# Weights rounded onto the e4m3 grid by TensorE in PSUM instead of by GpSimd and VectorE

## The reference

```python
u = jnp.einsum('bsd,hd->bsh', x, W_in) + b_in            # x: layernorm of the input
def step(state, u_t):
    s = jnp.tanh(u_t + state * gamma + beta)
    return (s, s)
_, states = jax.lax.scan(step, init, jnp.swapaxes(u, 0, 1))
y = jnp.einsum('bsh,dh->bsd', states, W_out) + b_out
...
def _quantized_matmul(x, w, scale):
    wq = w.astype(jnp.float8_e4m3fn).astype(x.dtype)
    y = jnp.einsum('bsi,io->bso', x, wq)
    return y * scale
gate = jax.nn.silu(_quantized_matmul(x, gate_w, gate_scale))
up = _quantized_matmul(x, up_w, up_scale)
return _quantized_matmul(gate * up, down_w, down_scale)
...
x = x + _layernorm(_L0_attn_ref(_layernorm(x), ...))
x = x + _layernorm(_L0_ffn_ref(_layernorm(x), ...))
```

## Time and profile before

| | |
|---|---|
| median of 3 runs | 625.39 us (625.18 to 625.69) |
| the profiled execution | 625.78 us, its span 624.0 us |
| TensorE busy | 528.8 us, 85% |
| VectorE busy | 481.0 us, 77% |
| ScalarE busy | 310.6 us, 50% |
| GpSimd busy | 240.4 us, 39% |
| mean granted TensorE clock | 0.937 |

### The profile page before, as it was taken

The page is one execution under the profiler, slowest core; times in us unless marked ns, Lnnn a source line. Parts: engine busy times, 40 slices in busy tenths (PEclk is TensorE's granted clock), DMA queues, the critical chain, the costliest instruction groups (busy, mean ns, idle before and its releaser), DMA issues.

```text
span 624.0 us, 9844 instructions
## 1 busy us (share of the span) xinstructions
PE 528.8 (85%) x2880; PEld 449.0 (72%) x2880; DVE 481.0 (77%) x1832; ACT 310.6 (50%) x1442; POOL 240.4 (39%) x320
## 2 busy tenths in 40 slices
PE   4655232878999999999999999999999992999993
PEld 4644211568977998789878987799779971798992
DVE  4999997999778667966787679767886678675734
ACT  1354423365554755576546654665466544452330
POOL 2776672555224222422333332422342224243532
PEclk9957757789999999999999999999999996999997
DMA  7453440301010200110012001100001000100000
GB/s 235 128 171 123 124 141 29 90 29 52 1 35 1 69 1 1 35 67 2 1 34 69 1 2 34 56 14 0 2 3 65 2 0 2 67 2 2 1 35 34
DMA packets 16598, 27.47 MB, mean 44 GB/s; under 512 B 2336, under 2 KB 4512, under 8 KB 16544
## 3 DMA queue, kind: packets, MB, share of 16 engines
q1 hardware_dynamic: 16544, 26.84, 13.7%
HBM read 22.63 MB, written 4.19 MB: 43 GB/s over the span
## 4 chain that ended last, share of the span: by engine, by line
DVE 57%; ACT 21%; PE 14%; issue 3%; DMA 1%; SPq 1%; POOL 1%; POOLq 0%; DVEq 0%; ACTq 0%
DVE recur L634 23%; ACT pairs L922 10%; PE gate_up L528 7%; ACT pairs L909 4%; DVE fused L728 4%; ACT sigm L942 4%; DVE gated L721 3%; PE wide L553 3%; DVE peaks L780 3%; ACT fused_hi L957 3%; PE wide L493 2%; DVE rounder_own L776 2%; DVE y L675 2%; DVE z L793 2%; DVE x_in L658 2%
## 5 line engine op out<-in xcount | busy, mean ns | idle before, releaser
L922 ACT ACTIVATE pairs<-recur 128x16 f32<-128x16 f32 x1024 | 191.2, 187 | 249.5 <-DVE recur L634 247.1
L634 DVE TENSOR_TENSOR_SCAN recur<-recur,pairs 128x32 f32<-128x32 f32 x1024 | 234.4, 229 | 101.5 <-ACT pairs L922 100.1
L1025 POOL TENSOR_TENSOR fused_lo<-fused,fused_hi 128x256 fp32r<-128x256 f32 x96 | 71.1, 741 | 180.5 <-ACT fused_hi L957 180.4
L468 PE MATMUL wide<-x_norm_t,w_in_sb 128*128 128x256 f32 x448 | 106.6, 396 | 17.5 <-ACT pairs L909 13.2
L482 PE MATMUL wide<-w_out_sb,pairs 128*128 128x512 f32 x224 | 101.3, 606 | 22.1 <-DMA w_out_sb<-w_out_t 22.1
L468 PEld LDWEIGHTS wide<-x_norm_t,w_in_sb 128*128 128x128 f32 x448 | 87.6, 199 | 34.6 <-ACT pairs L909 15.4
L482 PEld LDWEIGHTS wide<-w_out_sb,pairs 128*128 128x128 f32 x224 | 65.5, 297 | 51.8 <-DMA w_out_sb<-w_out_t 22.5
L528 PE MATMUL gate_up<-x_hi,gate_q 128*128 128x256 f32 x384 | 96.8, 285 | 1.0 <-DVE fused L728 0.6
L528 PE MATMUL gate_up<-x_lo,up_q 128*128 128x256 f32 x384 | 96.0, 283 | 0.0
L528 PE MATMUL gate_up<-x_hi,up_q 128*128 128x256 f32 x384 | 95.6, 282 | 0.0
L528 PE MATMUL gate_up<-x_lo,gate_q 128*128 128x256 f32 x384 | 94.9, 281 | 0.0
(11 more groups left out here) (75 smaller groups left out, 640.2 us busy)
## 6 DMA issues: line engine op xcount, KB each, us to landing
x_in<-x SPq DMA_DIRECT2D x16, 256.0 KB, 3.1
x_res<-x SPq DMA_DIRECT2D x16, 256.0 KB, 3.1
out<-z SPq DMA_DIRECT2D x14, 256.0 KB, 2.4
raw_own<-gate_w SPq DMA_DIRECT2D x10, 256.0 KB, 2.8
raw_own<-down_w SPq DMA_DIRECT2D x9, 256.0 KB, 2.7
w_in_sb<-w_in_t SPq DMA_DIRECT2D x4, 512.0 KB, 6.8
raw_own<-up_w SPq DMA_DIRECT2D x8, 256.0 KB, 2.7
w_out_sb<-w_out_t SPq DMA_DIRECT2D x8, 256.0 KB, 2.9
```

The lines of the kernel that those rows point to most:

```text
L468: ins = eng.matmul(wide[bank][:, jj * TOK:(jj + 1) * TOK], w_in_sb[:, k, j * P:(j + 1) * P], x_norm_t[:, k, :], start=(k == 0), stop=(k == ...
L634: eng.tensor_tensor_scan(preact[:, part(h), :].rearrange("p c k -> p (c k)"), factors[:, part(h), :].rearrange("p c k -> p (c k)"), pairs[ ...
L922: eng.activation(pairs[:, (n * T + t) % RING, part(h), 0], preact[:, part(h), 1], ACT.Tanh).then_inc(s_state[h], 1)
L1025: eng.tensor_tensor(fused_lo[:, f, :], fused[:, f, :], fused_hi[:, f, :].bitcast(F32), ALU.subtract).then_inc(s_fused_lo, 1)
```

## The change

R is made by VectorE as before, but from `powers` (two slots in the memory of `x1`) into a float32r `rounder`. The rounding itself goes to TensorE: `round_weights` adds three products in one PSUM bank, identity x raw piece in float32, identity x R and minus identity x R in float32r (`signed_ident`, written once by ScalarE). ScalarE copies the bank to the weights in two halves (`take_weights`), at `TAKE_BEHIND` = 4 and 5 places behind the matmuls' place, which is 1.5 behind the piece's fourth VectorE place. Three banks take turns. A raw slot is loaded again when TensorE has done its piece. VectorE keeps four instructions for every piece, GpSimd none. Pieces 0 to 3 now stand in the prologue (their matmuls at places 0 to 0.3 of block 0), 4 to 32 in block 0 and 33 to 35 in block 1 (VectorE places 1 to 21); the guard on gate and up moves to places 32 to 35 of block 1 and that on down to 39, 40, 43, 49. With the same rule for free places, piece 4 has VectorE places 1, 2, 3, 6, piece 5 has 7, 11, 12, 13, piece 6 has 14, 15, 20, 21, and from 22 on each piece has four places in a row up to 125.

```diff
-        PIECES_START, PIECES_FIRST = 6, 27
+        PIECES_START, PIECES_FIRST = 4, 33
...
-                piece_at[i] = [next(slots) for _ in range(4 if by_pool(i) else 8)]
+                piece_at[i] = [next(slots) for _ in range(4)]
...
-        GUARD_GATE_UP = [next(second_slots) for _ in range(4)]
         lay_pieces(PIECES_FIRST, NP, second_slots)
-        GUARD_DOWN = [next(second_slots) for _ in range(4)]
+        free = [s for s in second_slots if s >= GUARD]
+        GUARD_GATE_UP, GUARD_DOWN = free[0:4], free[4:8]
+
+        def round_place(i):
+
+            return piece_at[i][3] + 1.5 if i >= PIECES_START else 0.1 * i
...
-                    if i >= RAW and by_pool(i - RAW):
-                        eng.wait_ge(s_pool_converted, pool_pieces(i - RAW + 1))
-                    elif i >= RAW:
-                        eng.wait_ge(s_dve_converted, 2 * (i - RAW + 1 - pool_pieces(i - RAW + 1)))
+                    if i >= RAW:
+                        eng.wait_ge(s_rounded, i - RAW + 1)
...
+            def round_weights(first, end):
+
+                for i in range(first, end):
+                    yield round_place(i)
+                    bank = round_banks[i % NRB]
+                    if i == 0:
+                        eng.wait_ge(s_signed_ident, 2)
+                    eng.wait_ge(s_rounder, 4 * i + 4)
+                    if i >= NRB:
+                        eng.wait_ge(s_converted, 2 * (i - NRB + 1))
+                    eng.matmul(bank, ident[:, :], raw[i % RAW], start=True, stop=False)
+                    eng.matmul(bank, signed_ident[:, 0, :], rounder[i % RAW], start=False, stop=False)
+                    eng.matmul(bank, signed_ident[:, 1, :], rounder[i % RAW], start=False, stop=True
+                               ).then_inc(s_rounded, 1)
...
                 if n == 0:
                     strands.append(project_first_u(1, FIRST_U["u"]))
+                    strands.append(round_weights(0, PIECES_FIRST))
...
+            def take_weights(first, end):
+                for i in range(first, end):
+                    for half in range(2):
+                        yield round_place(i) + TAKE_BEHIND + half
+                        if half == 0:
+                            eng.wait_ge(s_rounded, i + 1)
+                        eng.copy(pieces[i][1][:, halves(half)], round_banks[i % NRB][:, halves(half)]
+                                 ).then_inc(s_converted, 1)
```

More of the change, by code:

```diff
@@ L69 @@
 CHAIN_BEHIND = 0.6
+GUARD = 30
+TAKE_BEHIND = 4
 LAG = 3
@@ L185, in recurrent_sandwich_kernel @@
         raw = [raw_own[:, r, :] for r in range(OWN)] + [z[:, 0, :]]
-        rounder = [rounder_own[:, r, :] for r in range(OWN)] + [z[:, 1, :]]
+        rounder = [rounder_own[:, r, :] for r in range(OWN)] + [
+            fused_lo[:, 0:2, :].rearrange("p f t -> p (f t)")]
+        powers = [x1[:, r, :] for r in range(2)]
+        signed_ident = fused_hi[:, 0, :].rearrange("p (s c) -> p s c", s=2)
         stats = {w: sb(f"stats_{w}", [P, batch, 2, nc.vector.BN_STATS_DIM]) for w in "xyrz"}
@@ L257, in recurrent_sandwich_kernel, with last_rounded_in @@
         s_last_ready = sem("s_last_ready")
[L259 to L266, removed]
+        round_banks = [gate_up[NG - 1][:, :, :].rearrange("p v t -> p (v t)"), wide[2][:, :], wide[3][:, :]]
+        NRB = len(round_banks)
+        def last_rounded_in(bank):
+            return max(i for i in range(NP) if i % NRB == bank) + 1
         def halves(h):
@@ L537, in down_products @@
                 if n == 0:
[L538 to L542, removed]
+                    eng.wait_ge(s_converted, 2 * (GATE_UP_PIECES + i + 1))
                     if i == DOWN_IN_TIME:
@@ L783, in convert @@
                     eng.wait_ge(s_rounder, 4 * i + 3)
[L784 removed]
+                    eng.tensor_scalar(rounder[i % RAW], powers[i % 2], LEAST_NORMAL, ROUNDING_CONSTANT, ALU.max,
                                       ALU.mult).then_inc(s_rounder, 1)
[L786 to L794, removed]
[L795 to L800 removed]
             def guard_weights(which, places, first, end, poisoned):
@@ L816, in guard_weights @@
                 eng.wait_ge(s_guard_step, 4 * which + 3)
-                eng.wait_ge(s_dve_converted, 2 * (end - pool_pieces(end)))
+                eng.wait_ge(s_converted, 2 * end)
                 eng.scalar_tensor_tensor(out=poisoned, in0=guard[:, 2:3], scalar=0.0, in1=poisoned.bitcast(F32),
@@ L957, in high_parts @@
                     eng.copy(fused_hi[:, f, :], fused[:, f, :]).then_inc(s_fused_hi, 1)
-            weave(warm_up(), *[copy_x(0, b, FIRST_BEFORE) for b in range(batch)], first_u(0, FIRST_BEFORE["u_copy"]))
+            weave(warm_up(), sign_identity(), *[copy_x(0, b, FIRST_BEFORE) for b in range(batch)], first_u(0, FIRST_BEFORE["u_copy"]))
             for n in range(NB):
@@ L1044, in tail @@
                 return strands
-            def round_weights(first, end):
-                for i in range(first, end):
-                    if not by_pool(i):
-                        continue
-                    yield piece_at[i][3]
-                    src, dst = raw[i % RAW], pieces[i][1]
-                    eng.wait_ge(s_rounder, 4 * i + 4)
-                    eng.tensor_tensor(src, src, rounder[i % RAW], ALU.add).then_inc(s_pool_rounded, 1)
-                    eng.wait_ge(s_pool_rounded, pool_pieces(i) + 1)
-                    eng.tensor_tensor(dst, src, rounder[i % RAW], ALU.subtract).then_inc(s_pool_converted, 1)
-            weave(prepare(), *[root("x", 0, b, FIRST_BEFORE["x_whole"][b]) for b in range(batch)],
-                  round_weights(0, PIECES_START))
+            weave(prepare(), *[root("x", 0, b, FIRST_BEFORE["x_whole"][b]) for b in range(batch)])
             for n in range(NB):
```

38 lines of the change are left out of this document (20 added, 18 removed).

## The result

| | before | after |
|---|---|---|
| median | 625.38 us (625.14 to 625.84, 10 runs) | 627.19 us (626.75 to 628.55, 10 runs) |
| ratio of the medians | | 1.0032, 95% interval 1.0024 to 1.0040 |
| the profiled execution | 625.78 us, span 624.0 us | 627.5 us, span 625.7 us |
| TensorE, VectorE busy | 528.8 and 481.0 us | 573.7 and 447.2 us |
| ScalarE, GpSimd busy | 310.6 and 240.4 us | 330.0 and 166.8 us |

The account below looks back on a forecast made before the run. The bound was the recurrence between VectorE and ScalarE, lengthened by GpSimd's rounding. From 625.8 us, -3.3 for gains less TensorE queue waits, +3.6 for half clock, +0.3 for longer first matmuls: 626.0 us, range 621.5 to 631.0.

Parts of the forecast that it names:

- first scan: Start of block 0: scan 0 at 21.2 us, when ScalarE's copies of the first inputs end, 4.6 us earlier.
- step 6: Block 0: piece 3 waits for its bank behind ScalarE's copies, so scan 7 starts at 31.8; 2.0 us lost.
- projections, steps 51, 55, 63, 71: Block 0: ScalarE's copies wait for pieces queued on TensorE among block 1's input projections; 9.2 us in all.
- steps with two ScalarE copies: Block 0, places 74 to 77: four input copies meet two weight copies, costing 0.3 us.
- block 1, step 12: y: Block 1: block 0's first product y stands before piece 33 on TensorE, whose copy is late; 2.9 us lost.
- block 1, guard: Block 1, places 32 to 35: weight guard beside a GpSimd residual add; 0 to 0.93 us, taken as 0.5.
- block 1, GpSimd's exit: Block 1: without GpSimd's rounding the longer steps shrink from 8.7 to 1.75 us, so 7.0 us go.
- that rival: VectorE writes float32r at half rate, 9 us more over 29 instructions in block 0: 635 us; chance 0.05.
- three pauses: TensorE idle before pieces 3, 6 and 35; half clock after each 7 in 10, costing 1.6, 1.9, 1.9 us.
- The forecast's case: Two of TensorE's three pauses are followed by the half clock, 3.6 us: range 624 to 628 us, chance 0.36.
- The second rival (clock up): TensorE's clock stays up through the pauses: 622.4 us; chance 0.22.
- One mark: Block 0's sign of a wrong forecast: waits of ScalarE for TensorE under 12 us in all.

Follow-up runs that it names:

- the last run: The changed kernel run once more, unchanged, which gave its second profile: 627.15 us, ratio 1.0032.
- the kernel with all moved: Against the kernel with projections apart and later copies: fifth slot, copies of pieces 0 to 3, second group's quads, y and last two pieces' copies moved; 606.64 us, ratio 0.9705.

## Why the prediction was right or wrong

The forecast was 626.0 us, with 621.5 to 631.0 around it, and slower as the likeliest sign; it came out at 627.19. The mechanism was the one forecast, and most of the long steps stand where they were put. But that the total is off by only 1.2 us is partly luck: without the clock, the sum was 622.8 us for the profiled execution (625.8 - 3.3 + 0.3), where 627.5 less the clock's 1.25 is 626.2; it was 3.4 us too low, and the clock took 2.3 less than the 3.6 I gave it. Each term, in the profiled execution (us above a plain step where it is a step):

| step of the prediction | worked out | measured |
|---|---|---|
| first scan | at 21.2 | at 22.25 |
| 128 plain steps | 61.6 | 61.9 |
| the 14 long steps gone | all | all |
| step 1: piece 4's load | 5.2 | 5.03 |
| step 6 | 2.0 | 2.26 |
| step 12: quad before piece 4 | 1.7 | 1.72 |
| projections, steps 51, 55, 63, 71 | 2.0 + 2.8 + 2.2 + 2.2 = 9.2 | 2.18 + 2.66 + 2.11 + 1.80 = 8.7 |
| steps with two ScalarE copies | 0.3 | 1.7 (ten) |
| step 26, block 0 | 0.2, 1.9 more at half clock | 1.5; 0.27 with the pause filled |
| block 1, step 0 | 0 | 1.0 |
| block 1, step 12: y | 2.9 | 2.1 |
| block 1, transposes and copies | 0.4 | 0.6 |
| block 1, guard | 0.5 | 0 |
| block 1, GpSimd's exit | -7.0 | -6.2 |

**Right.** That GpSimd held VectorE: shown by the kernel without its rounding (of the amount that I let go with it, the 0.1 us of step 127 stays in every kernel). That the same amount would come back as waits for TensorE, place by place: the six steps of block 0 that wait for a piece came within 0.4 us each, from nothing but durations and the order in the program. Scan 2 was to start at 27.4 and started at 28.25, the late first scan included. That writing float32r costs VectorE nothing: 0.41 us for L809, so that rival fell.

**Mis-sized.** First, the start: 21.2 took the copies' end from a trace in which it didn't matter. The first scan of the kernels with the change came between 20.93 and 22.32 us. In this profile the first quads took 6.67 us, where the kernel before shows 5.73 in the same place (first after, then before):

```profile
9.64 6.67 PE L457 MATMUL wide<-x_norm_t,w_in_sb 128*128 128x128 f32 x32 [0.74 <-ACT x_norm_t L904]
9.51 5.73 PE L449 MATMUL wide<-x_norm_t,w_in_sb 128*128 128x128 f32 x32 [0.80 <-ACT x_norm_t L879]
```

Within these 32 records the matmuls first follow each other at 0.21 us, then at 0.11. The change of pace comes at 15.6 us here and at 13.5 in the kernel before, and over the kernels with the change the first scan goes with it: at 20.93 to 21.07 us where 13 or 14 records come 0.21 apart, at 22.25 to 22.32 where 25 or 26 do. It isn't that the weights come late, as I expected before the last run: TensorE waits for none of them in this profile, and in one of the others only (0.24 us). Matmuls of this shape are 0.21 us apart in the second profile too where the granted clock is 0.50, but here the clock's record says 1.00, so what sets the pace at the start stays open. In the kernel before, VectorE's work on pieces 4 and 5 lay over it. Second, ScalarE: I looked for weight copies beside input copies only at 74 to 77, though the earlier trace rows show what two copies do to a step. The other eight steps (19, 20, 27, 28, 52, 60, 67, 68) are at 0.15 to 0.19 each; the kernel with one product has the same ten. Third, the last piece's two copies have place 130.5, beyond the block, and were emitted right behind the block's last tanh, before TensorE was done:

```profile
105.52 0.40 PE L518 MATMUL wide<-rounder_own,fused_hi 128*128 128x512 f32 x1
...
105.95 0.65 ACT L891 CAST down_q<-wide 128x256 fp32r<-128x256 f32 x2 [0.57 <-PE wide L518]
```

I had taken a place as something that runs on from block to block; it cost 1.0 us, and the kernel with all moved, whose last copies stand in block 1, doesn't have it. The other way went y (0.8 less than worked out) and the guard: its one-element instructions were not held beside GpSimd at all, so of my 0 to 0.93 the nothing was right.

**The clock.** I gave each of three pauses 7 in 10 and 1.6 to 1.9 us. The prices held roughly: 1.6 for the first (0.6 and 1.0 on two steps), 0.8 to 1.3 for the second, 1.5 for the third. How many fall isn't fixed by the program: one in one profile, three in the other. The forecast's case, two of them, was in neither. Over the seven profiles of kernels with such pauses (the kernel after twice, the pause before piece 6 filled, copies later, a fifth slot, and the two with projections apart), those of 2.59 to 2.71 us were followed by the half clock in 7 cases of 10 and those of 2.27 and 2.28 in 3 of 7, so the chance that I gave was about right for the first two and high for the third, which came out at 2.28 us and not 2.5. With one, my sum gives 622.8 + 1.9 = 624.7 us for that execution, and it took 627.5. The missing 2.8 us are the start (1.05), the double copies (1.4), block 1's step 0 (1.0), less gained by GpSimd's exit (0.8) and 0.5 behind block 1, together 4.75; against them stand y (0.8), the guard (0.5) and the clock's smaller price (0.65), 1.95. The other rows differ by less and nearly cancel.

The second rival (clock up) rested on the Trainium skill (TensorE: Matmul & The Clock Gate, HAM oscillation), which warns only of idle gaps longer than these. In the second profile the pauses of 2.71, 2.62 and 2.27 us were each followed by the half clock. The measurement decides: gaps of this size can cost it.

One mark that I had set was too tight: waits of ScalarE for TensorE under 12 us in all were to be wrong, and they are 10.0 at the pieces and 1.5 at the transposes, so by that sign the forecast would have failed though the long steps stood where it had put them. The six steps with a wait at a piece are lengthened by 12.7 us, more than the waits, mostly since at step 6 the wait is 0.64 and the rest of its 2.26 is the row of copies of pieces 0 to 3.

What stays open: what decides in which executions a pause is followed by the half clock; which of the moves of the last kernel gave how much of its last 10.3 us, since five came together; what sets the pace of the first matmuls; and whether step 26 opens in the last kernel with the quad at a place that the input copy needn't wait for.

## What to carry to other kernels

When an engine that works in program order gets more work and another one's critical queue waits for its results, write out that order and price each wait: what stands in front, less the slack. If the work in a stretch is more than its time, only distance helps; if one long item stands before a deadline, only slack helps; where both hold, as here, each alone is worth little (4.1 and -0.8 us), and the two together, with each group in halves, gave 10.3. Write out every condition of such a wait as well, also that a buffer may be overwritten: the quad that was moved behind the transposes made step 26, with the copy that overwrites its input, 1.5 us longer. A change that moves a cost from one engine to another may look like nothing (+0.3%), and still be the step that makes a faster kernel possible (-3%) once the deadlines are set anew.

## What the runs showed of the hardware that I had not expected

- TensorE at half clock after short pauses, in some executions of a program and not in others. Over seven profiles, pauses of 2.59 to 2.71 us were followed by it in 7 cases of 10, pauses of 2.27 and 2.28 us in 3 of 7.
- The first matmuls of an execution at 0.21 us each in place of 0.11, until 12.8 to 15.6 us in the profiles of kernels with the change, while the clock's record says 1.00.
- Less work can mean a slower engine: with one product per piece TensorE was busy for 18.5 us between 72 and 105 us, not 27.9 as in the kernel after, and its mean clock there was 0.59, not 1.00. The wait behind it, at step 12 of block 1, became 1.4 us longer.
- An instruction of one element on VectorE beside GpSimd's residual add isn't held (0.15 us each for L820 and L824 beside an add of 1.26), while 256 and 512 wide ones beside GpSimd take 1.33 to 1.52 us.
- Two copies by ScalarE in one step, of 256 columns both or of 256 and 128, cost the recurrence 0.15 to 0.19 us; one costs nothing.
